# First attention of a fused Trainium2 kernel: a third stack buffer, one row-maximum unit per slot four slots ahead, the normalisation chain regrouped, and ring units of 512 columns

## The reference

```python
xg = x.reshape(b, GROUPS, c // GROUPS, n)              # 8 groups, n = 1024
xn = (xg - mean) * jax.lax.rsqrt(var + EPS)            # group norm, times norm_w plus norm_b
qkv = jnp.einsum('oc,bcn->bon', qkv_w, xn) + qkv_b[None, :, None]
attn = jnp.einsum('bhdn,bhdm->bhnm', q * scale, k * scale)   # 8 heads of 16 channels
attn = jax.nn.softmax(attn, axis=-1)
out = jnp.einsum('bhnm,bhdm->bhdn', attn, v).reshape(b, c, n)
out = jnp.einsum('oc,bcn->bon', proj_w, out) + proj_b[None, :, None]
return out.reshape(b, c, h, w) + x_in
```

## Time and profile before

| what | value |
|---|---|
| runs of the kernel | 5554.0 us median of three, 5553.28 to 5566.23 |
| span of the profiled execution | 5548.6 us |
| PE, DVE, ACT, POOL busy over the span | 87%, 65%, 54%, 18% |
| first attention, first to last exponential | about 93 to 2122 us |

### The profile page before, as it was taken

How to read it: one execution, slowest core, us unless ns; L and a number is a source line. 1 busy time by engine, 2 the same in 40 slices (tenths; PEclk the granted TensorE clock), 3 DMA queues, 4 the chain that set the end, 5 groups by cost and what they waited for, 6 DMA issues and landing times.

```text
span 5548.6 us, 81822 instructions
## 1 busy us (share of the span) xinstructions
PE 4842.2 (87%) x25633; PEld 2616.5 (47%) x25633; DVE 3586.2 (65%) x7699; ACT 2987.7 (54%) x5420; POOL 1021.9 (18%) x1348
## 2 busy tenths in 40 slices
PE   5888888888888886957888888888899999999999
PEld 1222222222222221336777877787755555555554
DVE  6677777777777762555665656555576676766765
ACT  2655565665655653414555555556755455455552
POOL 2212112121222112202333333333210000000000
PEclk7999999999999998979999999999999999999999
DMA  2522222222222211223545454544321111111112
GB/s 84 144 70 81 81 70 70 70 73 78 73 89 82 66 45 38 29 68 106 165 140 163 141 162 147 157 146 129 106 61 45 50 48 45 50 46 47 52 45 75
DMA packets 406297, 477.10 MB, mean 86 GB/s; under 512 B 87640, under 2 KB 249648, under 8 KB 403760
## 3 DMA queue, kind: packets, MB, share of 16 engines
q1 hardware_dynamic: 372128, 424.84, 25.4%
q0 software_dynamic: 20576, 35.55, 2.3%
q10 hardware_dynamic: 13168, 11.48, 0.8%
HBM read 308.54 MB, written 145.57 MB: 82 GB/s over the span
## 4 chain that ended last, share of the span: by engine, by line
PE 33%; DVE 15%; issue 3%; DVEq 3%; ACT 2%; ACTq 0%; SPq 0%; DMA 0%
PE n_ps_f L2153 4%; PE n_ps_f L2146 4%; PE n_ps_xy L1801 3%; PE n_ps_h L1791 3%; PE n_ps_c L2193 2%; PE n_ps_h L2205 2%; PE n_ps_f L2140 2%; PE n_ps_f L1649 2%; PE n_ps_xy L2209 1%; DVEq L2025 1%; DVE n_stats L971 1%; DVE n_xln L983 1%; PE n_ps_f L995 1%; PE n_ps_h L2209 1%; DVE n_down_weights L2024 1%
## 5 line engine op out<-in xcount | busy, mean ns | idle before, releaser
L597 ACT ACTIVATE a_probs<-ps_b 128x512 f32<-128x512 f32 x2048 | 1111.0, 594 | 794.8 <-PE ps_b L693 782.0
L454 DVE TENSOR_REDUCE a_negmax<-ps_a 128x1 f32<-128x1024 f32 x1024 | 1206.1, 1219 | 378.9 <-PE ps_a L637 369.3
L637 PE MATMUL ps_a<-a_k_stack,a_q_stack 96*128 96x512 bf16 x2048 | 634.6, 396 | 178.8 <-DVE a_negmax L454 89.9
L693 PE MATMUL ps_b<-a_q_stack,a_k_stack 99*128 99x512 bf16 x2048 | 673.6, 391 | 68.2 <-ACT a_probs L597 30.9
L1604 ACT ACTIVATE n_hidden<-n_ps_h,n_b 128x128 f32<-128x128 f32 x1472 | 420.2, 374 | 339.1 <-PE n_ps_h L1791 338.3
L706 PE MATMUL ps_o<-a_probs,a_v_ones 128*32 128x512 f32 x4096 | 562.0, 622 | 0.2 <-ACT a_probs L597 0.2
L637 PEld LDWEIGHTS ps_a<-a_k_stack,a_q_stack 96*128 96x128 bf16 x2048 | 146.1, 99 | 732.2 <-DVE a_negmax L454 468.9
L1801 PE MATMUL n_ps_xy<-n_down_weights,n_hidden 128*128 x2944 | 410.7, 284 | 78.9 <-ACT n_xy L1618 72.8
L693 PEld LDWEIGHTS ps_b<-a_q_stack,a_k_stack 99*128 99x128 bf16 x2048 | 196.2, 100 | 487.8 <-ACT a_probs L597 251.5
L1801 PEld LDWEIGHTS n_ps_xy<-n_down_weights,n_hidden 128*128 128x128 f32 x2944 | 369.1, 196 | 117.0 <-issue 112.8
L1791 PE MATMUL n_ps_h<-n_xy,n_up_weights 128*128 128x128 f32 x2944 | 399.8, 279 | 3.6 <-issue 1.8
(11 more groups left out here) (346 smaller groups left out, 7532.8 us busy)
## 6 DMA issues: line engine op xcount, KB each, us to landing
n_up_weights<-in_L_ffn_W_dram SPq DMA_DIRECT2D x368, 256.0 KB, 2.7
n_up_weights<-score_scratch SPq DMA_DIRECT2D x512, 128.0 KB, 2.9
split_scratch<-a_pieces SPq DMA_DIRECT2D x180, 256.0 KB
a_q_stack<-split_scratch SPq DMA_DIRECT2D x128, 192.0 KB, 3.7
a_k_stack<-split_scratch SPq DMA_DIRECT2D x128, 192.0 KB, 4.1
rows_scratch<-n_zero SPq DMA_DIRECT2D x16, 1472.0 KB, 10.5
outs_scratch<-n_xy SPq DMA_DIRECT2D x176, 128.0 KB, 1.9
n_xg<-rows_scratch SPq DMA_DIRECT2D x80, 256.0 KB
```

The source lines that it names most:

```text
L454: dve.tensor_reduce(negmax[:, b, t:t + 1], bank, axis=AX.X, op=ALU.max, negate=True).then_inc(ring_read, 1)
L597: act.activation(probs[:, m % PROBS, 512 * k:512 * k + 512], ps_b[:, k, :], ACT.Exp).then_inc(b_exp, 1)
L637: last = pe.matmul(bank[:, cols], q_stack[0:KS, h, 128 * t:128 * t + 128], k_stack[0:KS, h, cols], start=True, stop=True)
L693: pe.matmul(ps_b[:, k, :], k_stack[:, h, 128 * t:128 * t + 128], q_stack[:, h, 512 * k:512 * k + 512], start=True, stop=True).then_inc(b_u ...
```

## The change

The change does the following.

- A third stack buffer. The last four images' place in `u_cols` serves as one more group's stack until image 15. The groups of all images go round over three buffers (`stacks`), so a group's load waits for the group three before it. `store_image` sends images 12 and 13 to DRAM (`held_scratch`), from where `load_held` brings them back in image 15.
- The pieces are stored in four slots instead of six (8 DMAs an image, not 12), and loaded in six DMAs a group of 32 partitions x 4 heads x 1024 (not eight of 96 x 1024); the order of the products within the 96 rows changes to allow it. All six DMAs count on one semaphore for each buffer.
- `maxima` puts exactly one A unit in every slot, and it stands `LEAD` = 4 slots before the slot that has its number. The first four of the next image's second group come in slots 60 to 63; the prologue does four more.
- PE's `body` changes its order: in an even slot the slot's first ring unit, B, W (now in slots 0 and 2 of a quad), then the other units; in an odd slot B, then the units.
- The norm's chain on DVE is shorter: products are fused, and the Newton iteration has two instructions a step instead of three. It is spread over slots: `stats`, `moments`, `sums`, `affine`, `norm`.
- `qk`, `v`, `project`, `take`, the first piece, `norm2` and the statistics go in halves of 512 columns, and `turn2` in quarters, each in its own slot. `o_up` and `o_out` are one semaphore a half.
- POOL does the first `shift_pieces` of the second group before `divide`. SP issues the next image's first stack load ahead of both shifts of the second group.

The diff, cut to its core:

```diff
-def group_affine(dve, scale, shift, group, sums, sums_read, width, small, eps):
+def group_variance(dve, scale, group, sums, sums_read, width, small, eps):
 
     dve.tensor_scalar(group[:, :], sums, 1.0 / width, None, ALU.mult).then_inc(sums_read, 1)
     dve.drain()
-    dve.tensor_tensor(small[:, 0:1], group[:, 0:1], group[:, 0:1], ALU.mult)
+    dve.scalar_tensor_tensor(small[:, 0:1], group[:, 0:1], group[:, 0:1], group[:, 1:2], ALU.mult, ALU.subtract)
     dve.drain()
-    dve.tensor_tensor(small[:, 1:2], group[:, 1:2], small[:, 0:1], ALU.subtract)
+    dve.tensor_scalar(small[:, 1:2], small[:, 0:1], 0.0, eps, ALU.min, ALU.subtract)
     dve.drain()
-    dve.tensor_scalar(small[:, 1:2], small[:, 1:2], 0.0, eps, ALU.max, ALU.add)
+    dve.tensor_scalar(scale.bitcast(I32), small[:, 1:2].bitcast(I32), -0.5, 1597463007.0 - 2.0 ** 30, ALU.mult, ALU.add)
+    dve.tensor_scalar(small[:, 2:3], small[:, 1:2], 0.5, None, ALU.mult)
     dve.drain()
-    rsqrt(dve, scale, small[:, 1:2], small[:, 2:3])
-    dve.scalar_tensor_tensor(shift, group[:, 0:1], -1.0, scale, ALU.mult, ALU.mult)
+
+
+def newton_step(dve, scale, small):
+
+    dve.scalar_tensor_tensor(small[:, 3:4], scale, scale, small[:, 2:3], ALU.mult, ALU.mult)
     dve.drain()
-
-
-def attention_phase(nc, sems, handles, B, io, const, const_in, band_dram, u_cols, gn2, x1_dram, split_dram, sums_dram, conv):
+    dve.scalar_tensor_tensor(scale, small[:, 3:4], 1.5, scale, ALU.add, ALU.mult)
+    dve.drain()
+
...
+        PRODUCTS = ((0, 0), (1, 1), (1, 0), (0, 1), (0, 2), (2, 0))
+        STORED = ((0, 1, 0, 2), (0, 1, 2, 0))
+        PAIRED = ((0, 1, 2), (0, 0, 2))
         KS = len(PRODUCTS) * D
         PIECES = 3
+        BUFFERS = 3
+        LEAD = 4
...
+        HOLD = B - 4
+        third = u_cols[:, HOLD:B, :, :].rearrange("p a c h -> p (a c h)").bitcast(BF16).rearrange("p (s j n) -> p s j n", s=2, j=J)
...
+        def stacks(i, g):
+
+            buffer = (G * i + g) % BUFFERS
+            if buffer < 2:
+                return q_stack[:, J * buffer:J * buffer + J, :], k_stack[:, J * buffer:J * buffer + J, :]
+            return third[0:KS + PIECES, 0, :, :], third[0:KS + PIECES, 1, :, :]
+
+        def stacked(i, g):
+
+            return stack_in[(G * i + g) % BUFFERS], STACKED * ((G * i + g) // BUFFERS + 1)
...
         def normed():
 
-            work = [(0, ("moments",)), (1, ("sums", 0)), (1, ("norm",))]
-            return work + [(4, ("qk", 0)), (6, ("qk", 1)), (9, ("v",))]
+            work = [(0, ("stats", 0, 0)), (1, ("stats", 0, 1)), (1, ("moments", 0)), (2, ("sums", 0))]
+            work += [(3, ("affine", 0, 0)), (3, ("affine", 0, 1)), (6, ("affine", 0, 2)), (7, ("norm",))]
+            work += [(8, ("qk", 0, 0)), (9, ("qk", 0, 1)), (9, ("piece", 0, 0)), (11, ("piece", 0, 1))]
+            work += [(12, ("qk", 1, 0)), (13, ("qk", 1, 1)), (13, ("piece", 1, 0)), (14, ("piece", 1, 1))]
+            return work + [(13, ("v", 0)), (22, ("v", 1)), (37, ("copy_v", 0))]
 
         def projected():
 
-            return [(2, ("take", 1)), (8, ("recip",)), (29, ("project",)), (30, ("moments2",)),
-                    (31, ("sums", 1)), (32, ("norm2",)), (34, ("turn2",))]
+            work = [(2, ("take", 1, 0)), (4, ("take", 1, 1)), (11, ("recip",)), (27, ("project", 0)), (29, ("project", 1))]
+            work += [(30, ("stats", 1, 0)), (32, ("stats", 1, 1)), (34, ("moments", 1)), (38, ("sums", 1))]
+            work += [(40, ("affine", 1, 0)), (40, ("affine", 1, 1)), (42, ("affine", 1, 2)), (46, ("norm2", 0)), (48, ("norm2", 1))]
+            return work + [(50 + 2 * k, ("turn2", k)) for k in range(4)]
 
         def maxima(ahead, g):
 
-            work = [(3 + n * 26 // QUAD, ("scores", ahead, g, n)) for n in range(QUAD)]
-            return work + [(18, ("shift", ahead, g, 0)), (30, ("shift", ahead, g, 1))]
+            work = [(n, ("scores", ahead, g, n)) for n in range(QUAD)]
+            return work + [(18, ("shift", ahead, g, 0)), (32, ("shift", ahead, g, 1))]
 
         def plan(front, back):
 
             by_slot = [[] for _ in range(SLOTS)]
-            for s, work in (projected() if back else []) + (normed() if front else []) + maxima(0, 1):
-                by_slot[s].append(work)
-            by_slot[QUAD + 2].append(("take", 0))
+            for s, work in maxima(0, 1):
+                if s >= LEAD:
+                    by_slot[s - LEAD].append(work)
             if front:
                 for s, work in maxima(1, 0):
-                    by_slot[QUAD + s].append(work)
+                    by_slot[QUAD + s - LEAD].append(work)
+                for s, work in maxima(1, 1):
+                    if s < LEAD:
+                        by_slot[SLOTS + s - LEAD].append(work)
+            for s, work in (projected() if back else []) + (normed() if front else []):
+                by_slot[s].append(work)
...
-                for s, slot in enumerate(PRODUCTS):
-                    sp.dma_start(split_dram[qk, :, s, :, :], pieces[:, qk, slot[qk], :]).then_inc(split_stored[qk], 16)
...
-            def load_stack(i, g, first=False):
-                for qk in range(2):
-                    if first:
-                        sp.wait_ge(first_stored[qk], 96)
-                    else:
-                        sp.wait_ge(split_stored[qk], i * 96 + 96)
-                for h in range(J * g, J * g + J):
-                    for qk, stack in enumerate((q_stack, k_stack)):
-                        sp.dma_start(stack[0:KS, h, :], split_dram[qk, h, :, :, :].rearrange("s d n -> (s d) n")).then_inc(stack_in[h], 16)
+                for slot, piece in enumerate(STORED[qk]):
+                    sp.dma_start(split_dram[qk, :, slot, :, :], pieces[:, qk, piece, :]).then_inc(split_stored[qk], 16)
+
+            def load_stacks(i, g):
+
+                if G * i + g >= BUFFERS:
+                    sp.wait_ge(b_up, (G * i + g - BUFFERS + 1) * (2 * QUAD))
+                for qk, stack in enumerate(stacks(i, g)):
+                    sp.wait_ge(split_stored[qk], (i + 1) * SPLIT)
+                    for n, slot in enumerate(PAIRED[qk]):
+                        sp.dma_start(stack[2 * D * n:2 * D * n + 2 * D, :, :],
+                                     split_dram[qk, J * g:J * g + J, slot:slot + 2, :, :].rearrange("j s d n -> (s d) j n")).then_inc(stacked(i, g)[0], 16)
...
             def body(prev, i, front, back, load):
-                if back:
-                    sp.wait_ge(b_up, i * (2 * SLOTS))
-                load_stack(i, 1)
...
                 if front:
-                    store_split(0, i + 1)
-                    store_split(1, i + 1)
+                    store_pieces(0, i + 1)
+                    store_pieces(1, i + 1)
+                    load_stacks(i + 1, 0)
                 send_shift(i, 1, 0)
                 send_shift(i, 1, 1)
                 if front:
-                    sp.wait_ge(b_up, i * (2 * SLOTS) + 2 * QUAD)
-                    load_stack(i + 1, 0)
+                    load_stacks(i + 1, 1)
+                    send_shift(i + 1, 0, 0)
+                else:
+                    load_held()
                 sp.wait_ge(xr_free, i + 1)
                 load_image(xr, *((prev, 1) if back else (0, 0)), xr_in)
                 if back:
                     store_image(prev)
                 if front:
-                    send_shift(i + 1, 0, 0)
                     send_shift(i + 1, 0, 1)
...
             for i in range(B - 1):
                 if i:
                     split(i + 1)
+                shift_pieces(i, 1, 0)
+                if i:
                     divide(i - 1)
-                shift_pieces(i, 1, 0)
                 shift_pieces(i, 1, 1)
                 shift_pieces(i + 1, 0, 0)
...
-                front, n = kind != "last", 0
+                n = 0
                 for m, works in enumerate(bodies[kind]):
-                    n = run(works, kind, i, n)
+                    run(works, kind, i, n, ("take",))
...
-                    if pending:
-                        first_piece(pending.pop())
+                    n = run(works, kind, i, n, ("qk", "piece", "copy_v"))
...
             def body(kind, i):
                 n, table = 0, units([work for slot in bodies[kind] for work in slot])
                 for m, works in enumerate(bodies[kind]):
-                    n = run(works, kind, i, n, table)
+                    units_of_slot = [work for work in works if work[0] in RING]
+                    if m % 2:
+                        shifted_scores(i, m)
+                        n = run(units_of_slot, kind, i, n, table)
+                        continue
+                    n = run(units_of_slot[:1], kind, i, n, table)
                     shifted_scores(i, m)
-                    if m % J < HALVES:
-                        if m >= J:
-                            weigh_values(i, m // J - 1, m % J)
-                        elif kind != "first":
-                            weigh_values(i - 1, G * NT - 1, m % J)
```

(5 more changed lines are left out.)

250 lines of the change are left out of this document (137 added, 113 removed).

## The result

The changed kernel takes 5305.5 us, median of 4 (5290.3 to 5316.2), against 5556.3 for the kernel before (5553.3 to 5566.2): a ratio of 0.9546, 95% interval 0.9527 to 0.9565. The forecast was 5250 with a range of 5190 to 5370, so the range held and the point lay 56 us too low.

A forecast was written before the change was run, and what follows sets the result against it. PE and DVE waiting for each other by turns, and both for a stack once an image, bound the kernel. Savings: middle images 267, image 0 21, image 15 14, closing run 2; 5548.6 - 304 + 5.4 = 5250 us, range 5190 to 5370.

The forecast's parts named there:

- middle images: Images 1 to 14 of the first attention: 109 us each instead of 128.1, saving 267 us in all.
- Pair of slots, 2.83: Two slots in the order B, A, A, B, W take 2.83 us if nothing waits; 32 pairs are 90.6.
- DVE in slots 0 to 7, 15.6: In slots 0 to 7 DVE needs 15.1 us, PE 11.3 + 0.2: 3.6 to 4 exposed; the slots take 15.6.
- first rival: DVE's lumps of other work are not hidden: 113 to 118 us an image, 5310 to 5385; chance 0.18.
- The clock: Rival: PE falls to 1.2 GHz in slots 0 to 7, 7 us more an image, 5355; chance 0.07.
- The chain: DVE's norm chain, 12 steps instead of 18, saves about 1.4 us a norm where nobody waits in the body.
- Slots 28 to 63: Rest of a middle image, 54.2 us; about 1 us of DVE's other work exposed in slots 30 to 56.
- Slots 8 to 15: 16.1 us with qk and v halves, plus 1.3 for ACT's bunched work and 0.5 in slot 9: 17.9.
- The stack, 48.5 us: The next image's first stack is in at 48.5 us, slot 28 asks at 51.5: three to spare, costing nothing.
- No gain, or slower: Rival: SP's wait for the keys' stores makes the stack 22 us or more later, gain gone; chance 0.06.
- Prologue: First A near 48, 4 us earlier; four more A units cost 4.7; together nothing.
- Image 0: The first image, without projection but starting at the lower clock, takes 106 us instead of 126.7, saving 21.

The follow-up runs named there:

- second transpose later: The changed kernel with the second transpose of the maxima one slot later, in slots 61 and 29 instead of 60 and 28: 5293.6 us, ratio 0.9525.
- mixed: The changed kernel with DVE copying q and k in even slots and the second transpose one slot later in slot 61 alone: 5265.6 us, ratio 0.9468.
- DVE's copies: The changed kernel with q and k halves in slots 8, 10, 12, 14 and copied by DVE instead of ACT: 5283.2 us, ratio 0.9510.
- spread run: The changed kernel with q and k halves in slots 8, 10, 12, 14 and their first pieces in the slots between: 5312.3 us, ratio 0.9557.
- run with two buffers: The changed kernel with A packed in slots 3 to 28 as before and no third buffer, loads still four heads each: 5728.4 us, ratio 1.0290.
- loads by head: The changed kernel with A in slots 3 to 28, two buffers, and the old stores and loads, one load a head: 5483.6 us, ratio 0.9869.
- A packed: The changed kernel with A put back into slots 3 to 28, no longer four slots ahead, three buffers kept: 5471.8 us, ratio 0.9836.
- A three slots ahead: The changed kernel with the second transpose one slot later and A three slots ahead instead of four: 5322.2 us, ratio 0.9567.
- long chain: The changed kernel with the old norm chain, 18 steps in one piece instead of 12 spread over three slots: 5410.8 us, ratio 0.9722.

## Why the prediction was right, and where it was off

The profiled spans differ by 245.7 us, the forecast said 304. The 58 between them: 14 middle images at 111.15 instead of 109 (30); image 0 at 116.4 instead of 106 (10); prologue 3.9 instead of 0; closing run 0.8 longer instead of 2 shorter (3); and 11.3 in the code behind attention. Image 15, measured to the end of its last exponential like the 108.9 before, took 95.0, in its range of 94 to 96. The middle image lies in the 105 to 113 that the forecast had named as its sign of being right.

- *Pair of slots, 2.83.* Right: 2.89, with W to B and A to A as taken. The 0.06 is 1.9 us an image.
- *DVE in slots 0 to 7, 15.6.* 14.3, DVE busy 13.11 of it: the exposed part was 2.8 and not 4. The first rival (lumps not hidden, 113 to 118 an image) did not come about; with the chain in one piece it did, at 118.8.
- *The clock.* PE stayed at 2.4 GHz almost through images 1 to 14 (1.00 on average). It fell twice, for 3.4 us each: at 540.2, behind one of the 14 waits of 1.46 us for the transpose, and at 997.6, behind a wait of 1.25 for the moments. The row is the first of them. The Trainium skill (TensorE: Matmul & The Clock Gate, psum-queue depth-cycling) says that frequent short idles at PSUM banks make the clock go up and down. This trace bears it out hardly at all: A's 70 waits for a reduction, up to 1.3 us, and 13 of the 14 of 1.46 us had no lower clock behind them.

```profile
540.20:543.60 3.40, 3.40 (x13) 0.71 (x13) 0.53 (x1) 1.03 (x3) 1.68 (x5) 0.50 0.00 0
```

- *The chain.* The step that failed: it called the chain "a path which nobody waits for in the body, since DVE has room". In one piece and at its old length it costs 7.6 us an image, as the run shows. DVE has 0.5 us of room a pair, and room over an image does not help against one piece of 4 us with a ring of two banks. That the sum was not hurt by it is luck in part: it put the shorter chain at nothing for the body, and was right only because it counted the change's own short pieces separately.
- *Slots 28 to 63.* Mis-sized by 4.0: the transpose behind its last reduction was given no wait. In slots 59 to 61 it costs 2.0 (second transpose later; mixed against DVE's copies). The 0.06 of 18 pairs is 1.1 more; the rest of the 4.0 was not traced.
- *Slots 8 to 15.* 18.4 against 17.9. The 1.3 for ACT's bunching was near, though in the spread run the cause is ACT's order and not its load.
- *The stack, 48.5 us.* It is in at 53 and not 48.5, and the three us to spare were none. The stores of the keys were issued from 917.7 (37.1 into the image, forecast 38.3), their load only from 927.2: stores and the queries' load shared the DMA engines, 200 GB/s in the window 913.3 to 933.0, where the forecast had given each the whole rate. The Trainium skill (SBUF — State Buffer, the DMA port swizzle) has 32-partition loads reach half of the ports. In the run with two buffers a group's 1.57 MB came in 9.5 us in this form; in the kernel before the old form's landed in 8.1 (991.97 to 1000.04). The sign agrees; the old form has 96 partitions, and other traffic was not kept apart.
- *No gain, or slower.* The wait for a whole stack is real, 16.5 us an image in the run with two buffers, which is slower than before. The third buffer hides it. But the forecast also held the third buffer to be what removes the stall of the kernel before, and that is not so: with loads by head the stall was gone with two buffers (122.5 us either way).
- *Prologue.* First A at 50.2 and not 48. The window 40 to 50, stores and load together, moved 232 GB/s at a DMA share of 0.88, against 87 and 0.23, which agrees with the fast rate that the forecast took for the stores. The four more A units cost 5.5 (first exponential at 91.4 with A packed, 96.9 here) and not 4.7.
- *Image 0.* Slots 40 to 55, beside the stores of the band rows, took 31 us against 24 later. ACT issues these stores, and the trace shows it held up by that: 1.1 to 3.5 us for each of the seven from slot 40 on, where each took 0.52 at this place in the kernel before. The next exponentials stand behind, and B behind them. Why an issue takes longer is not shown; the DMA engines were busier (share 0.85 in 150 to 180, before 0.66). The rows are from the changed kernel, the last from the kernel before. The image also starts at half clock, but so did the old one.

```profile
187.40 3.52 ACTq L620 DMA_DIRECT2D band_scratch<-u_cols  x1
191.62 1.09 PE L748 MATMUL ps_b<-a_q_stack,a_k_stack 99*128 99x512 bf16 x2 [1.86 <-ACT a_probs L664]
...
96.90:104.00 7.10, 5.89 (x16) 1.95 (x15) 5.46 (x13) 4.01 (x8) 0.00 (x0) 0.50 0.00 0
...
186.38 0.52 ACTq L556 DMA_DIRECT2D band_scratch<-u_cols  x1
```

- *The code behind attention* is the same in all 14 kernels, yet its profiled time goes from 3375.3 (DVE's copies) to 3391.4 us (A three slots ahead), before 3376.5 and after 3387.8, with no relation to the edits; at the two ends the granted clock over it is 0.96 and 0.95. The 11.3 is taken as this scatter.

## What to carry to other kernels

With a ring of two banks, engines had hardly any lead over each other: count what each needs slot by slot, not over the stretch. A piece of work in one go makes the others wait beyond the slack of its own slot, and here the half clock behind that wait cost more than the wait.

Put a unit that needs another engine's result where other work, as long as that result takes, lies between, and look at what an in-order engine has queued behind such a wait. A third buffer is worth what it lets start earlier; test it apart from the new order and the new form of loads that come with it.

## What the runs showed that was not expected

A wait of 2.23 us in the long chain was followed by a granted clock of 0.50 over 5 us, and one of 5.68 by A at 1.86 us for four matmuls. In the changed kernel, of 14 waits of 1.46 us one was followed by 3.4 us at 0.50, and the mean stayed 1.00 over 1556 us.

The form with one wait for four heads together (six loads, 9.5 us) made 16.5 us an image against the form with a wait for each head, with two buffers. That is more than any edit of the order cost.

The issue of a store of band rows held ACT for up to 3.52 us in the changed kernel and for 0.52 in the one before, with PE waiting behind.
